# One attention layer with four experts: every token through all experts, against tokens sorted into 11 tiles of one expert each

## What is computed

```python
q, k, v = (src @ Wq + bq), (src @ Wk + bk), (src @ Wv + bv)     # 16 heads of 8
attn = softmax(q k^T / sqrt(8)) v @ Wo + bo
x = layer_norm(src + attn, ln1_g, ln1_b)
keys = (x @ router_w + router_b)[..., 0]
expert_idx = remainder(floor(keys), 4)
for e in range(4):
    h = relu(x @ W1[e] + b1[e])                                 # 128 -> 512
    y = h @ W2[e] + b2[e]                                       # 512 -> 128
    ff_out = ff_out + where(expert_idx == e, y, 0)
return layer_norm(x + ff_out, ln2_g, ln2_b)
```

## Time and profile before

| | us |
|---|---|
| median of 3 runs | 4973.37 |
| lowest and highest | 4970.12, 4986.09 |
| the profiled execution's own time | 4982.11 |
| its span | 4980.2 |
| stream layer: first maxima of batch 0 | 2246.7 |
| store of the result issued | 4971.15 |

### The profile page before, as it was taken

One profiled execution on the slowest core, in us unless ns is written; L12 is line 12 of the kernel. 1 busy time (PEld: TensorE's weight loads), 2 busy tenths in 40 slices (PEclk: granted clock), 3 DMA queues, 4 the chain that ended last, 5 costly groups with the idle time before them and its releaser, 6 DMA issues.

```text
span 4980.2 us, 95171 instructions
## 1 busy us (share of the span) xinstructions
PE 4242.2 (85%) x38296; PEld 1782.1 (36%) x38296; DVE 3201.3 (64%) x4725; ACT 2869.0 (58%) x5344; POOL 1099.7 (22%) x1246
## 2 busy tenths in 40 slices
PE   4888867778787677847999999999999999999995
PEld 2334334334343444531233333333222222434343
DVE  4777534444444377618977776767879998686831
ACT  2767622221312355415876667677988987676761
POOL 2221001010100023231233232322121124050413
PEclk7999988788887888857999999999999999999997
DMA  2222001010000000011110101010111210111000
GB/s 77 57 58 57 10 15 23 21 22 1 22 2 0 7 1 1 1 55 31 42 40 15 40 15 40 15 40 15 47 34 28 53 47 16 39 26 29 15 2 17
DMA packets 100295, 133.96 MB, mean 27 GB/s; under 512 B 48194, under 2 KB 60994, under 8 KB 99348
## 3 DMA queue, kind: packets, MB, share of 16 engines
q1 hardware_dynamic: 99860, 127.92, 10.4%
HBM read 63.50 MB, written 54.00 MB: 24 GB/s over the span
## 4 chain that ended last, share of the span: by engine, by line
PE 66%; DVE 17%; ACT 5%; issue 5%; POOL 3%; DMA 2%; SPq 2%; POOLq 0%; DVEq 0%; ACTq 0%
PE ps L1058 15%; PE ps L1031 9%; PE ps L1088 6%; PE ps L1043 6%; DVE stream_max_pieces L1236 5%; PE ps L1135 5%; PE ps L544 3%; PE ps L1754 2%; PE ps L503 2%; PE ps L2445 1%; DVE mamba_conv_sum L2740 1%; PE ps L254 1%; SPq L820 1%; PE ps L1077 1%; PE ps L524 1%
## 5 line engine op out<-in xcount | busy, mean ns | idle before, releaser
L1236 DVE TENSOR_REDUCE stream_max_pieces<-ps 128x2 f32<-128x1024 f32 x1536 | 1808.9, 1217 | 414.2 <-PE ps L1043 408.9
L1153 ACT ACTIVATE stream_probs<-ps 128x512 f32<-128x512 f32 x3072 | 1655.8, 597 | 488.3 <-PE ps L1031 469.5
L1058 PE MATMUL ps<-stream_probs,stream_v 128*16 128x256 f32 x12288 | 987.4, 394 | 20.5 <-issue 19.8
L1043 PE MATMUL ps<-stream_k_stack,stream_q_stack 48*128 48x512 bf16 x3072 | 645.0, 394 | 97.7 <-DVE stream_max_pieces L1236 64.1
L1031 PE MATMUL ps<-stream_q_stack,stream_k_stack 51*128 51x512 bf16 x3072 | 657.9, 395 | 13.7 <-ACT stream_probs L1153 9.3
L683 DVE TENSOR_REDUCE alibi_max_pieces<-ps 128x2 f32<-128x1024 f32 (+3 forms) x384 | 355.4, 952 | 141.5 <-PE ps L528 132.1
L1058 PEld LDWEIGHTS ps<-stream_probs,stream_v 128*16 128x16 f32 x12288 | 202.9, 94 | 653.0 <-issue 430.8
L624 ACT ACTIVATE alibi_probs<-ps 128x512 f32<-128x512 f32 (+3 forms) x768 | 333.9, 492 | 178.1 <-PE ps L509 142.9
L1031 PEld LDWEIGHTS ps<-stream_q_stack,stream_k_stack 51*128 51x128 bf16 x3072 | 173.3, 93 | 725.3 <-ACT stream_probs L1153 582.6
L308 POOL CAST stream_negmax_parts<-stream_negmax_t 128x32 bf16<-128x32 f32 x96 | 20.3, 212 | 1440.4 <-DVE stream_negmax_t L1225 1405.4
L1088 PE MATMUL ps<-stream_x1T,stream_w 128*128 128x512 f32 x512 | 282.6, 642 | 0.0
(11 more groups left out here) (417 smaller groups left out, 5367.6 us busy)
## 6 DMA issues: line engine op xcount, KB each, us to landing
stream_q_terms_dram<-stream_q_parts SPq DMA_DIRECT2D x72, 256.0 KB
stream_k_terms_dram<-stream_k_parts SPq DMA_DIRECT2D x72, 256.0 KB
stream_q_stack<-stream_q_terms_dram SPq DMA_DIRECT2D x96, 192.0 KB, 4.1
stream_k_stack<-stream_k_terms_dram SPq DMA_DIRECT2D x96, 192.0 KB, 4.5
delta_v_shifted<-delta_v_padded SPq DMA_DIRECT2D x64, 158.0 KB, 3.6
alibi_q_terms_dram<-alibi_q_parts SPq DMA_DIRECT2D x24, 256.0 KB
alibi_k_terms_dram<-alibi_k_parts SPq DMA_DIRECT2D x24, 256.0 KB
alibi_q_stack<-alibi_q_terms_dram SPq DMA_DIRECT2D x32, 192.0 KB
```

The source lines that it names most:

```text
L1043: ins = e.matmul(c.ps[:, mbank(key) + r, :], qs[R, buf, pair, qt * P:(qt + 1) * P], ks[R, buf, pair, kh * 512:kh * 512 + 512], start=True, ...
L1058: ins = e.matmul(c.ps[32 * j:32 * j + 16, 7, Q], v[:, b % 2, kt, GH * g + j, :], pr[:, (u + j // 2) % RP, j % 2, Q], start=(n == 0 and k = ...
L1153: e.activation(pr[:, u % RP, r, :], c.ps[:, ebank(key), :], ACT.Exp, scale=SCALE).then_inc(s_ed, 1)
L1236: e.tensor_reduce(mx[:, j % 2, kh, 4 * pair + qt % 4, :], c.ps[:, mbank(key):mbank(key) + 2, :], AXX, ALU.max).then_inc(s_md, 1)
```

## The change

The tokens of a batch are sorted by expert, and each expert is applied to its own tokens only. An expert's tokens fill whole tiles of 128 rows, so 1024 tokens of four experts always fit in 8 + 3 = 11 tiles ("slots"), however they are spread. Step by step, for a moe batch:

- `rank`, position 36: from the masks PE counts, for each token, how many of the same expert come before it (one matmul with a triangular matrix of ones, eight with all ones); DVE makes of it each token's slot and each tile's expert, 12 small operations, and writes both as whole numbers.
- `scatter`, 53: POOL issues 8 indirect transfers of 64 KB (L1508) that put the rows of x1 at their slots in DRAM.
- `weights`, 54 for tiles 0 to 3, then two at a time at 85, 93, 101 and 109: POOL issues 11 indirect transfers (L1518) that fetch the weights of the tile's expert, 128 rows of 4624 bytes, into a ring of four buffers. W1, W2, b1 and b2 of an expert now lie in one DRAM tensor; they are no longer loaded at the start of the layer.
- `slots`, 70: SP loads all 11 tiles, 704 KB, into SBUF (L1566). `xsT`, 73 to 75: PE transposes them in three groups.
- `h`, 77 + 4j for tile j: four narrow f32 matmuls of 128x128 (L1181) and four Relus of 128x128. `w2`, 83 + 8i, at most 120: eight narrow matmuls for two tiles (L1189; four in the last), to which DVE adds b2.
- `ystore`, 123: SP stores 704 KB of expert outputs. `gather`, 127: POOL issues 8 indirect transfers (L1523) that fetch each token's row back. `stats`, 145: DVE adds them to x1 and takes the statistics, and `scale`, 146, on POOL.

x1 has two buffers now, since the second layer norm of one batch is taken among the units of the batch after the next one. At the start of the layer 448 KB of bias rows and 157 KB of constants are loaded in place of 704 KB of rows and the 2048 KB of weights. The bias passes on POOL are gone. In all there are 27 indirect transfers in a moe batch, 216 in the program.

```diff
-C_OB, C_X1, C_RW, C_B2, C_X = 1, 13, 14, 22, 35
-D_KEY, D_ST = 24, 32
-UNITS_E = ("xT", "q", "k", "v", "q_sums", "k_sums", "oT", "x1T", "h")
-UNITS_M = ("y", "w2")
+C_OB, C_X1, C_RW, C_X = 1, 13, 14, 13
+D_KEY, D_ST = 24, 34
+NWB = 4
+ET = TPB + NE - 1
+EW = 2 * NF * P + NF + D
+EB1, EB2 = 2 * NF * P, 2 * NF * P + NF
+RW_N = 2 * P + TPB + NE * NE + 3 * ET + 1
+UNITS_E = ("xT", "q", "k", "v", "q_sums", "k_sums", "oT", "xsT", "h")
+UNITS_M = ("y", "w2", "rank")
...
-        for k in range(2):
-            yield 30 + k, ("x1T", n, k)
         for k in range(3):
             yield 32 + k, ("key", n, k)
-        yield 35, ("bias2", n)
-        for i in range(2 * NE):
-            for j in range(NF):
-                yield 50 + 8 * i + j, ("h", n, i, j)
-            for p in range(2):
-                yield 56 + 8 * i + p, ("w2", n, i, p)
-        yield 116, ("stats", n, 1)
-        yield 117, ("scale", n, 1)
+        yield 36, ("rank", n)
+        yield 53, ("scatter", n)
+        for j in range(ET):
+            yield 54 if j < NWB else 85 + 8 * ((j - NWB) // 2), ("weights", n, j)
+        yield 70, ("slots", n)
+        for g in range(3):
+            yield 73 + g, ("xsT", n, g)
+        for j in range(ET):
+            yield 77 + 4 * j, ("h", n, j)
+        for i in range(ET // 2 + 1):
+            yield min(83 + 8 * i, 120), ("w2", n, i)
+        yield 123, ("ystore", n)
+        yield 127, ("gather", n)
+        yield 145, ("stats", n, 1)
+        yield 146, ("scale", n, 1)
...
-    w1 = c.sb(name + "_w1", [P, NE, NF * P], F32)
-    w2 = c.sb(name + "_w2", [P, NE, NF, D], F32)
-    rows = c.sb(name + "_rows", [P, 7 + NE, D], F32)
-    for tile, key in ((w1, "moe_w1"), (w2, "moe_w2"), (rows, "moe_rows")):
+    rows = c.sb(name + "_rows", [P, 7, D], F32)
+    rt = c.sb(name + "_route", [P, RW_N], F32)
+    for tile, key in ((rows, "moe_rows"), (rt, "moe_route")):
...
+    x1 = sb("x1", [P, 2, TPB, D])
+    wb = sb("expert_weights", [P, NWB, EW])
+    xs, xsT = sb("slots", [P, ET, D]), sb("slots_T", [P, ET * P])
+    hid = sb("hidden", [P, NWB, NF, P])
...
-            elif kind == "x1T":
-                e.wait_ge(s_pc, C_X * nth(n) + C_X1)
-                transposes(key, lambda t: x1[:, t, :])
+            elif kind == "rank":
+                e.wait_ge(s_dv, D_ST * nth(n) + D_KEY)
+                take_m(key)
+                out = c.ps[:, mbank(key), 0:NE * (TPB + 1)].rearrange("p (x t) -> p x t", x=NE)
+                e.matmul(out, earlier, mask[:, :, :], start=True, stop=False, skip_group_check=True)
+                for t in range(TPB):
+                    ins = e.matmul(out[:, :, t + 1:TPB + 1], ones, mask[:, :, t:t + 1].to_broadcast([P, NE, TPB - t]), start=False, stop=(t == TPB - 1), skip_group_check=True)
+                ins.then_inc(s_mf, 1)
...
+            elif kind == "xsT":
+                g = key[2]
+                if g == 0:
+                    e.wait_ge(s_xl, 16 * (nth(n) + 1))
+                take_e(key)
...
-                x, k, j = key[2] // 2, key[2] % 2, key[3]
-                e.wait_ge(s_ed, E.done(("x1T", n, k)))
-                wide(key, w1[:, x, j * P:(j + 1) * P], x1T[:, k * 512:(k + 1) * 512])
+                j = key[2]
+                e.wait_ge(s_ed, E.done(("xsT", n, j // 4)))
+                e.wait_ge(s_wl[j % NWB], weights_in(n, j))
+                take_e(key)
+                for f in range(NF):
+                    ins = e.matmul(c.ps[:, ebank(key), f * P:(f + 1) * P], wb[:, j % NWB, f * P:(f + 1) * P], xsT[:, j * P:(j + 1) * P], start=True, stop=True)
+                ins.then_inc(s_ef, 1)
             elif kind == "w2":
-                x, p = key[2] // 2, key[3]
-                e.wait_ge(s_ed, E.done(("h", n, key[2], NF - 1)))
+                tiles = [j for j in (2 * key[2], 2 * key[2] + 1) if j < ET]
+                e.wait_ge(s_ed, E.done(("h", n, tiles[-1])))
                 take_m(key)
-                for t in range(2):
-                    for j in range(NF):
-                        ins = e.matmul(c.ps[:, mbank(key), t * P:(t + 1) * P], hid[:, j, (2 * p + t) * P:(2 * p + t + 1) * P], w2[:, x, j, :], start=(j == 0), stop=(j == NF - 1))
+                for j in tiles:
+                    for f in range(NF):
+                        ins = e.matmul(c.ps[:, mbank(key), (j % 2) * P:(j % 2 + 1) * P], hid[:, j % NWB, f, :], wb[:, j % NWB, NF * P + f * D:NF * P + (f + 1) * D], start=(f == 0), stop=(f == NF - 1))
...
+                if k >= NWB:
+                    e.wait_ge(s_mf, M.done(("w2", n, (k - NWB) // 2)))
+                for f in range(NF):
+                    ins = e.activation(hid[:, k % NWB, f, :], src[:, f * P:(f + 1) * P], ACT.Relu, bias=wb[:, k % NWB, EB1 + f:EB1 + f + 1])
...
+                    cw.at((TPB + 1) * nth(n))
+                    e.wait_ge(s_yg, 16 * TPB * (nth(n) + 1))
+                    cw(e.tensor_tensor(x, x, xs[:, 0:TPB, :], ALU.add))
+                    cw.sync()
...
-                    step(e.tensor_tensor(weighed, rows[:, 7 + x:8 + x, :].to_broadcast([P, TPB, D]), mask[:, x, :].unsqueeze(2).to_broadcast([P, TPB, D]), ALU.mult))
-                    step(e.tensor_tensor(x1[:, :, :], x1[:, :, :], weighed, ALU.add))
-                assert cp.n == C_B2
+            elif kind == "scatter":
+                e.wait_ge(s_dv, D_ST * (nth(n) + 1))
+                e.wait_ge(s_zx, 16)
+                wait(e, s_xl, 16 * nth(n))
+                for t in range(TPB):
+                    e.indirect_dma_start(xd[:, :], bass.IndirectOffsetOnAxis(ap=posi[:, t:t + 1], axis=0), x1_of(n)[:, t, :], None).then_inc(s_sc, 16)
+            elif kind == "weights":
+                j = key[2]
+                if j == 0:
+                    e.wait_ge(s_rw, nth(n) + 1)
+                if j >= NWB:
+                    e.wait_ge(s_md, M.done(("w2", n, (j - NWB) // 2)))
+                elif nth(n):
+                    last = max(i for i in range(n) if plan.kind(i) == "moe")
+                    e.wait_ge(s_md, M.done(("w2", last, ET // 2)))
+                e.indirect_dma_start(wb[:, j % NWB, :], None, c.ins["moe_experts"], bass.IndirectOffsetOnAxis(ap=rowi[:, j:j + 1], axis=0)).then_inc(s_wl[j % NWB], 16)
+            elif kind == "gather":
+                e.wait_ge(s_yl, 16 * (nth(n) + 1))
+                e.wait_ge(s_ef, E.done(("xsT", n, 2)))
+                for t in range(TPB):
+                    e.indirect_dma_start(xs[:, t, :], None, yd[:, :], bass.IndirectOffsetOnAxis(ap=posi[:, t:t + 1], axis=0)).then_inc(s_yg, 16)
...
+        e.wait_ge(s_set, NSET)
+        e.dma_start(xd.rearrange("(j p) d -> p j d", p=P), xs[:, :, :]).then_inc(s_zx, 16)
...
+            if kind == "slots":
+                e.wait_ge(s_sc, 16 * TPB * (nth(n) + 1))
+                e.wait_ge(s_zx, 16)
+                wait(e, s_dw, (TPB + 1) * nth(n))
+                e.dma_start(xs[:, :, :], xd.rearrange("(j p) d -> p j d", p=P)).then_inc(s_xl, 16)
+            elif kind == "ystore":
+                e.wait_ge(s_md, M.done(("w2", n, ET // 2)))
+                wait(e, s_yg, 16 * TPB * nth(n))
+                e.dma_start(yd.rearrange("(j p) d -> p j d", p=P), xs[:, :, :]).then_inc(s_yl, 16)
...
+    r["moe_experts"] = np.ascontiguousarray(np.concatenate([m("W1"), w2, b1, b2], 2).reshape(NE * P, EW))
```

176 lines of the change are left out of this document (112 added, 64 removed).

## The result

| | before | after |
|---|---|---|
| median, us | 4974.4 (4 runs) | 4933.9 (4 runs) |
| lowest to highest | 4970.1 to 4986.1 | 4929.1 to 4941.1 |
| profiled execution, its span | 4982.1, 4980.2 | 4941.1, 4939.3 |
| first maxima of the stream layer | 2246.7 | 2246.9 |
| store of the result issued | 4971.2 | 4930.2 |

The ratio is 0.9916, with a 95% interval from 0.9894 to 0.9938: faster by 0.8%, some 40 us, where 99 to 100 were forecast. The profiled executions differ by 41.0, and all of it lies in the stream layer. The text compares with those.

What follows compares the result with a forecast made beforehand. PE, DVE and ACT were taken as full. Seven batches gain 45.3 - 20t each, the tail loses 20t - 17, the start gains 5: change -339 + 160t, -99 at t = 1.5, median 4874 us; 8-in-10 range 4780 to 5030.

Steps and rivals of the forecast that it cites:

- What bounds the kernel: Stream layer: PE, DVE and ACT full at 1.155 us a unit; insertions cost nearly their length, dense experts 68 us a batch.
- Expert arithmetic: Experts beside units: eleven h tiles 14.3, w2 groups 10.5, hand-offs and waits 3.1; 28 us instead of 68, 40 gained a batch.
- Rank: Rank group on PE and DVE among the units: matmuls 2, DVE's small steps 2.5, hand-offs 1.0; 5.5 us lost a batch.
- The price t: Time one indirect transfer holds POOL: 1.5 us taken, 1.1 to 1.9 the forecast's range at chance 0.44.
- Rival 1: POOL's indirect issues are dear, t above 2.12 us, so the kernel gets slower: 5082 us at 2.8; chance 0.22.
- what the new transfers stand in front of: Units 41 to 73: twelve issues delay maxima and slots; PE waits 12t - 6.4 us a batch, plus 2.7 for low clock.
- Weights hidden, nothing counted: Later tiles' weights, issued at 85 to 109: some 12 us of units and groups cover 2t + 4.5; no cost.
- Turn: Turn of the batch: store and eight gathers at 127 ahead of next input's POOL passes cost 3 + 8(t - 1.5) us.
- a sign of being wrong: Turn of a batch: growth by more than 5 us was named as evidence against the forecast.
- Tail: Last batch's experts, no units beside: 58.2 + 19t us instead of 73.6; 86.7 at t = 1.5, 13 lost.
- Layer start, 5 gained: Start of the layer: 704 KB of rows behind two 1024 KB tensors landed after 9.2 us, 674 KB alone 3.8; 5 gained.
- residual add: Add formerly inside the masked adds, now a DVE pass over 128x1024: about 1.2 us lost a batch.

Runs made afterwards that it cites:

- the paced kernels before the last: The changed kernel with indirect transfers spaced out: at late positions 4931.9 us; with slots loaded early 4864.1; with slots ahead of stores and weights waiting for them 4860.8.
- the one with direct rows: The changed kernel with scatter and gather each as one direct 512 KB transfer from SP, tokens in their own order, indirect weights kept: 4851.8 us, ratio 0.9733 against the change.
- the best version: The changed kernel with spaced indirect transfers, early slots, weights waiting for slots, and q and k stores behind the rows of maxima: 4809.7 us, ratio 0.9657 against the kernel before.

## Why the prediction was wrong

It had the sign and the range (4933.9 in 4780 to 5030), and a gain of 99 where 41 were measured.

1. *What bounds the kernel*: right. A PE group between units cost its own length, before and after. One reading was wrong: the x66 of the earlier trace rows counts units that are cut at the edges. 64 units take 75.6 us, 1.18 each and not 1.155; 70 take 82.7, and the dense experts cost 66 us a batch, not 68.
2. *Expert arithmetic, 40 a batch*: positions 48 to 120, which now hold all three transposes as well, were to be 37.9 us shorter (40 less 3 x 0.7). Without the stop they are 35.3 shorter on the mean of six batches (33.2 to 36.4); 1.7 of the 2.6 is that reading.
3. *Rank*: 5.5 forecast, 5.2 measured in batch 10's stretch (2.5 to 6.5 in the seven), with the wait for the key in it as before.
4. *The price t*: 1.27, inside 1.1 to 1.9 and below the 1.5 that I took. Rival 1, dear issues, did not come. Of what its page warns, the "DVE blocks DMA" box in "SBUF — State Buffer" of the Trainium skill, this kernel shows nothing: all 216 issues took 0.94 to 1.25 us, DVE busy or not. It is no test of the box either, for beside them DVE ran reductions, statistics, small steps and results out of PSUM, and no copy within SBUF. The estimate of 1.0 that I drew from "DMA: Bandwidth & Descriptors" (the anatomy of a transfer from GpSimd) of the Trainium skill is near the busy time of 0.96; from the pitch of 1.27 that holds POOL in a row it is as far off as my 1.5.
5. **The step that failed** is "what the new transfers stand in front of". I let twelve issues hold only the work queued behind them and priced that: PE was to stand still 12t - 6.4 at position 73. The place and the mechanism were wrong, since the run stops PE itself, in the very units that I counted as cover: 14.3 us a batch on the mean of seven, at 56 to 64 (40 to 56 in the last). The chain through SP was real but lay behind it, and showed (7.7 to 12.7 us, 8.4 in batch 10's stretch) once the stop was taken away. At the measured t my terms give 8.8 + 2.7 = 11.5. At the t of 1.5 that I had chosen they give 11.6 + 2.7 = 14.3, the measured size; that is luck: a t that was too high stood in for a stop that was not in the sum.
6. *Weights hidden, nothing counted*: their issue and use were hidden, but 2.3 MB of them together with the stores of the q and k parts held up a 3 KB write: a round of 6.0 us behind the stores alone took 10.2 to 14.3 (medians of four kernels), which the sum had no term for. In the change it took 5.4 to 7.0, as the stores were long issued; in the paced kernels before the last and in the one with direct rows it, or the slots' load in the same place, made the next wait.
7. *Turn*: 3 + 8(t - 1.5), 1.2 at the measured t; 5.0 to 7.6 measured, over the 5 that I had named as a sign of being wrong. Eight gathers are a run too, 9.8 us long, and stop PE.
8. *Tail*: from the key's last step (4818.9) to the statistics (4907.2) 88.3 us, where 73.6 were before: 14.7 lost, 13 forecast. Besides, the gathers of batch 10 stopped the last units for 7.3 us. DVE's small steps did not all cost 0.21: beside POOL's passes over 128x1024 three, which read two tiles in SBUF, took 2.15 to 2.27; in the other seven batches, with POOL idle, the same three took 0.17 to 0.19.

```profile
4825.80 2.15 DVE L1386 TENSOR_TENSOR stream_compared<-stream_route,stream_tile_counts 128x16 f32<-128x16 f32 x1
...
4907.24 1.65 DVE L1357 BATCH_NORM_STATS2 stream_stats<-stream_x 128x6 f32<-128x128 f32 x8
```

9. *Layer start, 5 gained*: 0. The first maxima stand at 2246.9, before at 2246.7, though 2.1 MB less are loaded; something else is last there, and I had not asked what.

In sum: from the first maxima of batch 1 to the last maxima passed 2369.4 us before and 2307.1 after, 62.3 gained where 107 were forecast. Of the 45 that are missing, the turns hold 16 (36.7 where 21 were forecast) and the experts' stretches 26 (11 of them because the last is counted only up to position 87); rank and residual add hold 3, and the stop none, by the luck of point 5. With 8 behind the last maxima and 5 at the start that makes the 58 us by which the forecast was off. At the measured t the same formula promises 136 us, 95 too many: 20 of the stop, 28 of the turns, 26 of the experts' stretches, 3 of rank and add, 13 behind the last maxima and 5 at the start. The half of it that belongs to runs of indirect transfers is what the experiments explain.

What stays open: whether PE's matmul itself is held during a run, or only the news of its end, and by what. The profile models a matmul's end, so the rows fit both, and no run here tells them apart. Nor was a pause shorter than one POOL pass of 1 us tried. Runs of two and three stand in the changed kernels without a visible stop: in the best version three gathers follow each other at one of the positions 11 to 13 of six stretches, and positions 8 to 16 take what they took before or 0.5 us less.

## What to carry to other kernels

Cost a run of indirect transfers not only by what waits behind it: put the run alone, with nothing waiting for it, into the old kernel and look at the engines beside it. Spread such issues between other passes of the same engine, but see that the last of them still lands before it is needed; where a stop goes, look at once for the wait that lay under it, for the gain shows only when that goes too. And a small write that a chain waits for belongs ahead of large stores and loads, whoever issues them.

## What the runs showed of the hardware

- An indirect transfer of 128 rows holds POOL 0.96 us, 1.27 in a row; a direct one from POOL 0.55, from SP 0.46 (eight in 3.66).
- Eight indirect ones in a row stop PE, ACT and DVE for 8.1 to 9.5 us beside plain units and 4.8 to 6.7 beside experts, twelve for 13.7 to 15.8 (mean granted clock 0.71 in those units), four for 2.4 to 4.8 and 0 to 0.7, threes and pairs not visibly; one in every two units costs 0.14 each. Eight direct ones, from SP or POOL, cost the units beside them nothing.
- Where POOL issued 88 transfers, of either kind, the result's store was issued 10.0 us after POOL's last pass (11.2 in the change with direct rows), with 44 transfers 6.5 us, with none 3.0 us, with the change's 216 4.9 us.
- 578 KB of weights in 128 rows land 5.9 us after issue (median of 88; 592 thousand bytes). A round of 3 KB writes took 3.6 us with nothing in front, 6.0 behind the stores of the q and k parts, 5.4 to 7.0 behind four weight loads, and 13.6 (median) behind both.
- DVE steps on 16 or 32 columns that read two SBUF tiles took 2.15 to 2.27 us beside a POOL pass on SBUF, and 0.17 to 0.19 with POOL idle.
